# A causal mask moved from TensorE's score product into VectorE's row maximum, in a single-core attention and feed-forward kernel

## The reference, cut to what matters

```python
scores = jnp.einsum('bhqd,bhkd->bhqk', q, k) / math.sqrt(HD)
causal = jnp.tril(jnp.ones((s, s), dtype=bool))
scores = jnp.where(causal[None, None], scores, jnp.finfo(scores.dtype).min)
attn = jax.nn.softmax(scores.astype(jnp.float32), axis=-1).astype(q.dtype)
ctx = jnp.einsum('bhqk,bhkd->bhqd', attn, v)
```

## Time and profile before

| | |
|---|---|
| median of three runs | 627.3 us (627.1 to 629.48) |
| the profiled execution, device time | 629.09 us |
| its span, first to last instruction | 627.3 us |
| PE busy | 582.9 us (93%) |
| PE weight loads busy | 436.8 us (70%) |
| DVE busy | 513.7 us (82%) |
| POOL busy | 417.7 us (67%) |
| ACT busy | 331.2 us (53%) |
| granted TensorE clock, mean | 0.962 |

### The profile page before, as it was taken

The page is one execution under the profiler, slowest core; times in us unless marked ns, Lnnn a source line. Parts: engine busy times, 40 slices in busy tenths (PEclk is TensorE's granted clock), DMA queues, the critical chain, the costliest instruction groups (busy, mean ns, idle before and its releaser), DMA issues. The chain is left out here.

```text
span 627.3 us, 10367 instructions
## 1 busy us (share of the span) xinstructions
PE 582.9 (93%) x3072; PEld 436.8 (70%) x3075; DVE 513.7 (82%) x670; ACT 331.2 (53%) x877; POOL 417.7 (67%) x420
## 2 busy tenths in 40 slices
PE   6999989999999999999999999999999999866664
PEld 4545668888887888788778878887888787534221
DVE  2874658988998899889979998998899887667894
ACT  2142465565565645655565556555655555206973
POOL 3004375997699669976986897699769976103674
PEclk9999999999999999999999999999999999996675
DMA  9921425423431341134224422431331121000012
GB/s 277 230 63 33 112 82 161 116 52 91 108 89 52 117 117 50 50 117 120 51 66 138 114 57 73 117 100 50 117 84 50 51 51 33 1 1 0 1 51 84
DMA packets 37787, 52.17 MB, mean 83 GB/s; under 512 B 11588, under 2 KB 19940, under 8 KB 37764
## 3 DMA queue, kind: packets, MB, share of 16 engines
q1 hardware_dynamic: 34692, 46.15, 28.0%
q10 hardware_dynamic: 2592, 4.53, 2.2%
q0 software_dynamic: 480, 1.22, 0.6%
HBM read 28.81 MB, written 2.10 MB: 49 GB/s over the span
## 5 line engine op out<-in xcount | busy, mean ns | idle before, releaser
L931 DVE SCALAR_TENSOR_TENSOR accT<-pair,so_now,accT 128x1024 f32<-128x1024 f32 x125 | 157.4, 1277 | 21.3 <-PE pair L1163 20.7
L917 DVE SCALAR_TENSOR_TENSOR raw_q<-pair,sc_now,raw_q 128x1024 f32<-128x1024 f32 x90 | 115.4, 1283 | 3.5
L1162 PE MATMUL pair<-ctx_hi,wo 128*128 128x512 f32 x256 | 104.9, 410 | 2.6 <-issue 1.5
L633 ACT ACTIVATE probs<-flow,negmax 128x128 f32<-128x128 f32 x248 | 87.5, 370 | 34.5 <-DVE negmax L882 34.5
L1162 PE MATMUL pair<-h_hi,wq 128*128 128x512 f32 x240 | 100.9, 421 | 1.8 <-ACT raw_q L676 1.7
L1163 PE MATMUL pair<-ctx_lo,wo 128*128 128x512 f32 x256 | 100.3, 392 | 0.0
L1163 PE MATMUL pair<-h_lo,wq 128*128 128x512 f32 x240 | 94.3, 393 | 0.0
L495 POOL TENSOR_TENSOR probs<-probs,rowinv 128x512 f32<-128x512 f32 x64 | 66.8, 1045 | 28.8 <-DVE rowinv L904 28.8
L476 POOL TENSOR_TENSOR qT<-rope_c,rope_s 128x512 f32<-128x512 f32 x62 | 79.5, 1283 | 4.4
L464 POOL TENSOR_TENSOR rope_s<-swap_q,consts 128x512 f32<-128x512 f32 x62 | 80.4, 1296 | 2.3 <-DMA swap_q<-raw_q 2.3
L464 POOL TENSOR_TENSOR rope_c<-raw_q,consts 128x512 f32<-128x512 f32 x62 | 78.6, 1290 | 0.6
(11 more groups left out here) (222 smaller groups left out, 1040.0 us busy)
## 6 DMA issues: line engine op xcount, KB each, us to landing
swap_q<-raw_q SPq DMA_DIRECT2D x62, 256.0 KB, 3.6
wq_i<-in_L_attn_qw_q SPq DMA_DIRECT2D x8, 1024.0 KB, 5.5
wo_i<-in_L_attn_qw_o SPq DMA_DIRECT2D x32, 256.0 KB, 2.7
swap_k<-raw_k SPq DMA_DIRECT2D x14, 256.0 KB, 3.6
wkv_i<-in_L_attn_qw_k SPq DMA_DIRECT2D x8, 256.0 KB, 3.8
wkv_i<-in_L_attn_qw_v SPq DMA_DIRECT2D x8, 256.0 KB, 4.0
out<-probsT SPq DMA_DIRECT2D x8, 256.0 KB, 2.0
stage<-in_x ACTq DMA_DIRECT2D x4, 256.0 KB, 5.4
```

What stands on the lines that cost most here:

```text
L633: e = act.activation(probs[:, 0, f, seq(b)], bank[:, seq(b)], ACT.Exp, bias=negmax[:, f, b:b + 1], accum_out=rowsum[:, f, b:b + 1])
L917: dve.scalar_tensor_tensor(out=into, in0=flat(pair[pair_of(h, (kind, j), last)][:, :, :]), scalar=sc_now[:, scale_slot(kind, h), j:j + 1], ...
L931: dve.scalar_tensor_tensor(out=a, in0=flat(pair[pair_of(h, (O, c), last)][:, :, :]), scalar=so_now[:, (h if c == 0 else h - 1) % 2, c:c + ...
L1162: pe.matmul(into[:, f, :], w, upper[:, half[f]], start=True, stop=False)
```

## The change

The table `tri_b` and the product L1148 are gone; the first score product now starts the bank. `maxima` no longer is one reduce. For each of the four sequences VectorE runs one `tensor_tensor_reduce`: it adds the fp32 mask `tri` to the scores, negates, writes the result to SBUF (`masked`, a half of `probs` that is not otherwise used in the loop) and keeps the minimum, which is the negated maximum. Ahead of the four stands a copy of one column (`seen_col`), which carries the waits. The exponentials read `masked` with scale -1 in place of the PSUM bank.

```diff
@@ maxima, on VectorE
             def maxima(n, f, last_head=False):
                 dve.wait_ge(scores_done, 2 * n + f + 1)
-                dve.tensor_reduce(negmax[:, f, :], per_seq(score_bank(f, last_head)), AX.X, ALU.max, negate=True).then_inc(negmax_done, 1)
+                wait(dve, seen, 2 * n + f)
+                dve.tensor_copy(seen_col[:, :], magic).then_inc(seen, 1)
+                for b in range(HB):
+                    ins = dve.tensor_tensor_reduce(out=masked[:, f, seq(b)], in0=score_bank(f, last_head)[:, seq(b)], in1=tri,
+                                                   scale=-1.0, scalar=-MASKED, op0=ALU.add, op1=ALU.min, accum_out=negmax[:, f, b:b + 1])
+                ins.then_inc(negmax_done, 1)
@@ exps, on ScalarE
-                    e = act.activation(probs[:, 0, f, seq(b)], bank[:, seq(b)], ACT.Exp,
+                    e = act.activation(probs[:, 0, f, seq(b)], masked[:, f, seq(b)], ACT.Exp, scale=-1.0,
                                        bias=negmax[:, f, b:b + 1], accum_out=rowsum[:, f, b:b + 1])
@@ scores, on TensorE
-                pe.matmul(bank, ident_b[:, :], on_each_seq(tri_b[:, :]), start=True, stop=False)
                 for b in range(HB):
                     t = seq(HB * f + b)
-                    mm = pe.matmul(bank[:, seq(b)], qT[:, par, t], kT[:, t], start=False, stop=(b == HB - 1))
+                    mm = pe.matmul(bank[:, seq(b)], qT[:, par, t], kT[:, t], start=(b == 0), stop=(b == HB - 1), skip_group_check=True)
                 mm.then_inc(scores_done, 1)
```

More of the change, by code:

```diff
@@ L69, in build @@
         ident, ones = consts[:, K_ID:K_ID + P], consts[:, K_ONE:K_ONE + P]
+        tri = consts[:, K_TRI:K_TRI + P]
         cos, sin = consts[:, K_COS:K_COS + P], consts[:, K_SIN:K_SIN + P]
@@ L73, in build @@
         ident_b = sb("ident_b", [P, P], BF16)
-        tri_b = sb("tri_b", [P, P], BF16)
         lora_mask = sb("lora_mask", [P, B])
@@ L103, in build @@
         sc_now = sb("sc_now", [P, 4, C])
+        seen_col = sb("seen_col", [P, 1])
         negmax = sb("negmax", [P, 2, HB])
@@ L131, in build @@
         diag = probsT[:, :, :]
+        masked = probs[:, 1, :, :]
         sc_nat = rope_c[:, 0, :]
@@ L187, in build @@
         pv_done, ctx_kept, ctx_split = sem("pv_done"), sem("ctx_kept"), sem("ctx_split")
+        seen = sem("seen")
         so_set, mask_made, table_set = sem("so_set"), sem("mask_made"), sem("table_set")
@@ L628, in early_wide, with exps @@
                                scale=sc_now[:, scale_slot(kind, n), 0:1]).then_inc(early_first, 1)
-            def exps(n, f, bank):
+            def exps(n, f):
                 act.wait_ge(negmax_done, 2 * n + f + 1)
                 for b in range(HB):
-                    e = act.activation(probs[:, 0, f, seq(b)], bank[:, seq(b)], ACT.Exp,
+                    e = act.activation(probs[:, 0, f, seq(b)], masked[:, f, seq(b)], ACT.Exp, scale=-1.0,
                                        bias=negmax[:, f, b:b + 1], accum_out=rowsum[:, f, b:b + 1])
@@ L701, in body @@
                         keep_values(g, 1)
-                    exps(n, 0, score_bank(0, last and h == 3))
+                    exps(n, 0)
                     if present(h, (Q, 0), first, last):
@@ L707, in body @@
                         drain_first(Q, n + 2)
-                    exps(n, 1, score_bank(1, last and h == 3))
+                    exps(n, 1)
                     if h < 2 and not last:
@@ L839, in _ @@
             dve.tensor_scalar(lora_mask[:, :], low_mask, 2.0, None, ALU.mult).then_inc(mask_made, 1)
-            dve.tensor_copy(tri_b[:, :], consts[:, K_TRI:K_TRI + P]).then_inc(consts_made, 1)
             dve.wait_ge(mask_made, 1)
@@ L1122, in _ @@
             pe.wait_ge(xT_dve, 4)
-            pe.wait_ge(consts_made, 2)
+            pe.wait_ge(consts_made, 1)
             turn_weights(0)
```

## The result

The changed kernel takes 631.19 us (median of 5 runs, 629.68 to 632.65) against 627.3 us before: a ratio of 1.0056 with a 95% interval of 1.0037 to 1.0075, so 2.3 to 4.7 us or 0.6% slower. The sign was forecast, the size was not: 647.4 us was expected, 20 us more, and 4 came.

A forecast was written before the change was run, and what follows sets the result against it. A ring of waits VectorE, GpSimd, ScalarE, VectorE was taken as the bound. Delay by the maxima 14.7, last head 1.4 and ScalarE's SBUF reads 4.0 made 20.1 us more: 647.4 us against 627.3, range 630 to 676.

The forecast's parts named there:

- the ring: Cycle of waits VectorE, GpSimd, ScalarE, VectorE in each head, claimed to pace the head at 14.8 us.
- the turn: One pass of the ring, from one head's first maximum on VectorE to the next head's: 14.82 us.
- What the change removes: 64 mask products on TensorE, 14.1 us of its time, none on the ring: costed as no gain.
- The cost M of the new maximum: On VectorE, a copy plus four pairs (128-column instruction and one-column read-out): M between 1.15 and 2.1 us, taken as 1.3.
- How M reaches the ring: Second exponentials wait for the second maximum, done 2M + 2.50 after O 3: mean delay 0.73 us in 20 heads, 14.7 us.
- break-even: Length of a maximum up to which the second exponentials are not delayed at h = 0 to 2: 0.9 to 0.98 us.
- the term for the last head: The last head's two maxima stand back to back with nothing to cover them: 1.4 us more.
- ScalarE's reading of SBUF: Exponentials read SBUF instead of PSUM, 0.032 us longer each, four on the ring in each of 31 heads: 4.0 us.
- the second: Rival: M at most 0.95, so the reciprocals' waits for exponentials absorb VectorE's growth; 628 to 633 us, chance 0.16.
- The first rival: Each read-out on VectorE waits for the pipeline to empty, M is 2.1: 686 us; range 663 to 686, chance 0.16.
- The third rival: TensorE is the bound, so each head gets 0.44 us shorter and the kernel faster: 613 us, chance 0.08.
- The signs to look for: Right: maximum about 1.3 us, second exponentials waiting for it. Wrong: exponentials directly behind Q 0, pairs far from 0.32 us.

The follow-up runs named there:

- e1: Kernel before without the mask product on TensorE and nothing in its place, scores left unmasked: 625.67 us, ratio 0.9990.
- e6: Changed kernel with a product of the old mask product's size run again ahead of the scores, its result overwritten: 631.41 us, ratio 1.0061.
- e7: Kernel before with GpSimd's copy of the output scale put behind the next head's first three rotary products instead of ahead of them: 622.37 us, ratio 0.9908.
- e5: Kernel before with two unused VectorE instructions over 256 columns ahead of each maximum, which then costs 1.26 us: 642.36 us, ratio 1.0236.
- e3: Kernel before with one unused VectorE instruction over 236 columns ahead of each maximum, to bring it from 0.59 to 0.90 us: 628.41 us, ratio 1.0031.
- e2: Kernel before with the exponentials reading a table of ones in SBUF instead of the score bank in PSUM: 631.40 us, ratio 1.0077.
- e4: Changed kernel with the masked scores written back over the score bank in PSUM, from where the exponentials read them: 630.93 us, ratio 1.0057.
- e9: e7 without the mask product on TensorE, scores left unmasked: 611.43 us, ratio 0.9746.

## Why the prediction was wrong, point by point

- **What bounds the kernel** (the ring, not TensorE): right. e1 and e6 show that the product is worth nothing in both kernels, e7 that GpSimd's wait was on the ring. "With TensorE close behind" was right too, closer than thought. But the turn was read at h = 1 and isn't the same at every head. At h = 0 VectorE's first `split_context` waits 0.62 us for ScalarE's context, so a part of that turn goes over the context. At h = 3, the longest head (15.20 us), GpSimd doesn't wait for O 3; from its second normalisation, which the second reciprocal releases, it works with hardly a gap. Timeline of GpSimd before:

```profile
307.53 1.04 POOL L495 TENSOR_TENSOR probs<-probs,rowinv 128x512 f32<-128x512 f32 x1 [0.74 <-DVE rowinv L904]
...
315.11 1.28 POOL L490 TENSOR_TENSOR kT<-raw_k,swap_k 128x512 f32<-128x512 f32 x1
316.37 0.19 POOL L524 COPY so_now<-so_cols 128x4 f32 x1
```

So a second chain, over GpSimd's own work, closes there at the same time as the one over VectorE's drains (first maximum at 316.14). Which of the two holds that head no run separates.

- **What the change removes, costed at no gain**: right (e1).
- **The cost M of the new maximum: the step that failed.** The prediction bounded a pair between 0.27 and 0.47 us and took 0.32; it is 0.21. The small instruction was well chosen, 0.20 between starts. The read-out was priced at 0.10, between tiny instructions in a row and tiny ones that wait for each other; it costs 0.01, below both, because it starts together with its successor. So M is 0.90 instead of 1.3, and even the lower bound of 1.15 was too high. The error was to take for the floor the distance of tiny instructions that each do work of their own; here the floor was zero.
- **How M reaches the ring**: right in form and numbers for the loop, shown by e5. But it is a threshold: with break-even at 0.9 to 0.98, the 0.4 us of error in M is the difference between 14.7 us and none. With M = 0.90 the prediction's own sum is 0 in the loop, 2 x 0.31 = 0.6 at the last head and 4.0 for ScalarE: 4.6, or 631.9 us. Measured are 631.19. A part of this closeness is luck, since the term for the last head isn't there: from the second reciprocal of head 29 to that of head 31 the traces have 22.45 us before, 22.36 changed and 22.46 in e3. There VectorE was idle for 0.81 us between the two maxima before, and the longer first one goes into that.
- **ScalarE's reading of SBUF**: right mechanism, and by e2 the whole of the result. Forecast were 0.13 us per head, the period shows 0.10 to 0.11. The size was partly luck: the rows of an exponential differ by 0.021 us (391 and 370 ns) and not by 0.032, but the starts differ by 0.04 to 0.05, and a head of h = 2 takes the delay up.
- **The rivals**: the second, growth that is covered, came true with its range of 628 to 633, at a chance of 0.16. I wrote that the rows of small instructions speak against it; they did for the instruction and had nothing to say on the read-out. The first rival is refuted by M = 0.90: an instruction of 0.28 us is followed after 0.21, its read-out included. The Trainium skill, page "VectorE: DVE Perf Modes", says in its section on the DRAIN that the next operation doesn't start until the pipeline is empty, and in the same section that an operation which isn't held starts earlier; the prediction left the second half out. The start 0.07 us before the row's end goes with the second half; how much of a row is the pipeline, no run here shows. The third rival is refuted by e1. (The first rival's sum counts 8 heads between groups where there are 7; that is 0.6 us of its 58.7.)
- **The signs to look for** did their work: exponentials that still follow Q 0 directly, a pair far from 0.32 us.

What stays open is where the rest of e3's 2 us lies. The traces can't say, because opening and end differ by as much from one execution to the next: the second reciprocal of head 4 starts at 145.34 us before, 144.52 changed and 143.92 in e3, and from that of head 28 to the end there are 128.09, 127.29 and 126.89 us. So the spans of the profiled executions (627.3, 628.3 and 625.0) differ by 1.0 and -2.3 us where the 24 heads between differ by 2.7 and 0.4.

## What to carry to other kernels

An engine that is busy for 99% of a stretch need not be the bound; follow one turn of the loop through its waits until it closes, and note for each instruction beside it how much later it could be. If a change lengthens something with slack, the result is zero up to a threshold and full price behind it, so the one number to be careful with is the one that is compared with the threshold, and a chance for "just under it" belongs in the forecast in proportion. And ask of each new operand where the next engine reads it from: here the whole cost that the runs could show was ScalarE's longer read of SBUF, which the change made in passing. Of the kernels that compute all of the reference the fastest was neither of the two but e7, 0.9% under before, by moving one waiting copy on GpSimd.

## What the runs showed of the hardware that was not expected

- The row minimum and its write-out by a custom VectorE instruction run as fast as a plain copy of 128 columns from PSUM: 0.21 us between starts against 0.20, with the read-out (82 ns in its own row) hidden behind the next instruction.
- With PSUM as its destination the same pairs are 0.25 us apart after the first, and the read-out's row is 0.14 us instead of 0.08 (e4).
- TensorE's busy share of 100 us was 99.7 where 14 us of its work were free and 99.8 where they were worth over 10 us (before and e7, with e1 and e9).
- An exponential over 128 columns with a row sum takes 391 ns from SBUF and 370 from PSUM, but between starts the difference is larger, 0.38 to 0.39 against 0.34 us (e2, e4).
